# Parts of Q and K after rotation: places of their own, three stores per block for six, first loads given out on two queues

## What is computed

```python
Q = rope((x @ qw).reshape(b, s, 16, 8)); K = rope((x @ kw).reshape(b, s, 16, 8))
V = (x @ vw).reshape(b, s, 16, 8)
score = einsum('bhqd,bhkd->bhqk', Q, K) / sqrt(8) - 1e10 * (1 - causal)
x = layernorm(x + merged(softmax(score - max) @ V) @ ow)
gates = top2_of_softmax(x @ router_w + router_b)       # four experts
x = layernorm(x + sum_e gates[e] * ((silu(x @ w1[e]) * (x @ w3[e])) @ w2[e]))
```

## Time and profile before

| | us |
|---|---|
| median of 3 runs | 496.91 (495.39 to 498.34) |
| the profiled execution's own time | 497.89 |
| its span in the trace | 496.2 |
| PE busy in the span | 416.2 (84%) |
| DVE busy | 313.3 (63%) |
| ACT busy | 267.1 (54%) |
| POOL busy | 190.2 (38%) |

### The profile page before, as it was taken

The page is one execution under the profiler, slowest core; times in us unless marked ns, Lnnn a source line. Parts: engine busy times, 40 slices in busy tenths (PEclk is TensorE's granted clock), DMA queues, the critical chain, the costliest instruction groups (busy, mean ns, idle before and its releaser), DMA issues.

```text
span 496.2 us, 7475 instructions
## 1 busy us (share of the span) xinstructions
PE 416.2 (84%) x2397; PEld 209.4 (42%) x2420; DVE 313.3 (63%) x1027; ACT 267.1 (54%) x377; POOL 190.2 (38%) x255
## 2 busy tenths in 40 slices
PE   5715473899898998989989888989999999999992
PEld 2302310222223222232222322327888788788781
DVE  3526374687887878878778786333556756765844
ACT  1220300557556576575755757676665575565560
POOL 3631320205215152151431513224565574665662
PEclk9957555799999999999999999889999999999996
DMA  6644544021122121221212100000000000000000
GB/s 230 190 125 120 159 100 122 13 63 47 20 65 50 47 61 24 65 49 40 60 33 64 41 3 0 3 0 1 2 0 2 21 1 1 22 1 2 22 0 21
DMA packets 46198, 23.47 MB, mean 47 GB/s; under 512 B 30320, under 2 KB 43248, under 8 KB 46160
## 3 DMA queue, kind: packets, MB, share of 16 engines
q1 hardware_dynamic: 46160, 23.00, 17.6%
HBM read 14.21 MB, written 8.59 MB: 46 GB/s over the span
## 4 chain that ended last, share of the span: by engine, by line
PE 58%; DVE 17%; SPq 7%; DMA 6%; ACT 5%; issue 4%; POOL 2%; POOLq 0%; DVEq 0%; ACTq 0%
PE o_bank L1055 12%; PE t_bank L1123 8%; PE bank L1123 8%; PE t_bank L1134 8%; DVE maxima L789 7%; PE t_bank L1038 6%; PE bank L1015 6%; PE small_bank L1015 3%; DMA q_op<-max_rows 3%; SPq L408 3%; DVE mg_w L785 2%; DVE mg_t L785 2%; DVE x_w L785 2%; SPq L367 2%; ACT num L628 2%
## 5 line engine op out<-in xcount | busy, mean ns | idle before, releaser
L628 ACT ACTIVATE num<-t_bank 128x1024 f32<-128x1024 f32 (+2 forms) x160 | 145.1, 939 | 110.1 <-PE t_bank L1038 108.8
L549 POOL TENSOR_TENSOR hid_lo<-num,q_op 128x512 fp32r<-128x512 f32 x64 | 83.0, 1300 | 60.9 <-ACT q_op L684 59.7
L518 POOL TENSOR_SCALAR_AFFINE_SELECT num<-num 128x512 f32<-128x512 f32 x64 | 40.3, 636 | 145.6 <-ACT num L628 145.5
L1015 PE MATMUL bank<-k_op,q_op 128*128 128x512 bf16 (+7 forms) x241 | 74.4, 338 | 22.8 <-DMA k_op<-k_scratch 10.8
L1055 PE MATMUL o_bank<-num,v_op 128*32 128x512 f32 (+3 forms) x768 | 84.5, 513 | 1.1
L1038 PE MATMUL t_bank<-q_op,k_op 64*128 64x512 bf16 (+3 forms) x384 | 59.8, 339 | 11.9 <-DMA q_op<-max_rows 10.2
L684 ACT ACTIVATE q_op<-num 128x512 fp32r<-128x512 f32 x64 | 40.5, 632 | 45.1 <-DVE num L916 44.7
L789 DVE TENSOR_REDUCE maxima<-bank 128x1 f32<-128x512 f32 x85 | 58.4, 688 | 7.9 <-PE bank L1015 4.5
L785 DVE CUSTOM_DVE_ANT_0 mg_t<-bank,resid 128x320 f32<-128x320 f32 (+6 forms) x85 | 37.9, 446 | 23.2 <-PE bank L1015 14.4
L1015 PEld LDWEIGHTS bank<-k_op,q_op 128*128 128x128 bf16 x255 | 23.2, 98 | 67.3 <-DVE maxima L789 20.8
L1038 PEld LDWEIGHTS t_bank<-q_op,k_op 64*128 64x128 bf16 x384 | 16.0, 93 | 76.6 <-issue 46.3
(11 more groups left out here) (132 smaller groups left out, 640.8 us busy)
## 6 DMA issues: line engine op xcount, KB each, us to landing
k_op<-k_scratch SPq DMA_DIRECT2D x32, 128.0 KB, 2.3
q_op<-q_scratch SPq DMA_DIRECT2D x64, 51.0 KB
q_scratch<-rope_part SPq DMA_DIRECT2D x24, 128.0 KB, 2.4
k_scratch<-rope_part SPq DMA_DIRECT2D x24, 128.0 KB, 2.4
w_raw<-in_w_all SPq DMA_DIRECT2D x6, 512.0 KB, 4.1
xT<-in_x_feat SPq DMA_DIRECT2D x4, 256.0 KB, 5.4
k_scratch<-k_op SPq DMA_DIRECT2D x4, 256.0 KB
q_op<-max_rows SPq DMA_DIRECT2D x64, 3.0 KB
```

Source lines behind the costliest of these rows:

```text
L518: pool.affine_select(out=tile, in_=tile, compare_op=ALU.is_ge, fill=0.0, base=0, pattern=[[0, GH], [1, P]], channel_multiplier=-1)\
L549: pool.tensor_tensor(hid_lo[:, m % HB, :], hid[:, m % HB, :], hid_hi[:, m % HB, :].bitcast(F32), ALU.subtract).then_inc(f_lo, 1)
L628: act.activation(num[:, t % PB, :, off:CH].rearrange("p (k i) t -> p i k t", i=2)[:, :, h:h + each, :], t_bank[k % TB][:, :, 0:each * (CH ...
L1015: pe.matmul(ring(s, step)[:, 0:width], q_op[u][:, pr, j, :, :].rearrange("p i q -> p (i q)"), k_op[u][:, pr, lo:lo + width], start=True, s ...
```

## The change

The three parts of each of the 8 blocks get places of their own, 24 in all, in the memory of `num` (three of its four slots), so no part waits for a store of an earlier block. ACT waits for all stores before the first exponential writes there. In DRAM the scratch tensors are laid out as (head and width) x product x token. The products of one part are then a slice with a step, and one DMA with a repeated source stores all copies of a part: three stores per block for six, of 3, 2 and 1 copies.

The rows of ones no longer go through DRAM: POOL fills both K buffers whole with ones, and the loads of K bring 48 rows for each head, four DMAs for two. The loads of Q bring 48 rows for 51. For groups 0 and 1 the rows of maxima are zero from the memset; from group 2 on each load of a head has a second DMA that brings three rows of zeros. The memset of the second Q buffer moves behind the last part, a memset of the second K buffer stands behind it, and the loads of group 1 wait for that.

For the first chunk, SP loads Q of two heads, and ACT hands out the loads of K and of the other two heads, behind part 1 of block 3. `STEADY` is now written out as a string of letters; the list of steps that comes out is the same, step for step.

```diff
-Q_PART = (0, 0, 1, 1, 2, 0)
-K_PART = (0, 1, 0, 1, 0, 2)
+Q_AT = ((2, 5, 1), (1, 6, 4), (0, 1, 1))
+K_AT = ((0, 3, 1), (3, 6, 2), (4, 5, 1))
...
-STEADY = stage_plan(True, True)
+STEADY = steady_plan(STEADY_ORDER)
...
-        q_dram = nc.dram_tensor("q_scratch", (B * H, QROWS, S), BF16).ap()
-        k_dram = nc.dram_tensor("k_scratch", (B * H, HR, S), BF16).ap()
+        q_dram = nc.dram_tensor("q_scratch", (B * H * DH, PRODUCTS, S), BF16).ap()
+        k_dram = nc.dram_tensor("k_scratch", (B * H * DH, PRODUCTS, S), BF16).ap()
+        z_dram = nc.dram_tensor("zeros", (PARTS, S), BF16).ap()
...
-        rope_part = [sb(f"rope_part{r}", [P, 2, CH], BF16) for r in range(PARTS)]
+        rope_part = num[:, 0:PB - 1, :, :].rearrange("p i h t -> p (i h t)").bitcast(BF16)\
+            .rearrange("p (n r t) -> p n r t", n=2 * CHUNKS, r=PARTS)
...
+        def load_q(eng, n, u, c, heads):
+            for h in heads:
+                pr, i = divmod(h, 2)
+                at = (n * GH + h) * DH
+                eng.dma_start(q_op[u][i * HR:i * HR + KROWS, pr, c * NB:(c + 1) * NB, i, :],
+                              q_dram[at:at + DH, :, c * CH:(c + 1) * CH].rearrange("d r t -> (d r) t"))\
+                    .then_inc(q_loaded[u][c], 16)
+                if n > 1:
+                    eng.dma_start(q_op[u][i * HR + KROWS:i * HR + QROWS, pr, c * NB:(c + 1) * NB, i, :],
+                                  z_dram[:, c * CH:(c + 1) * CH]).then_inc(q_loaded[u][c], 16)
+
+        def load_k(eng, n, u, c):
+            for h in range(GH):
+                pr, i = divmod(h, 2)
+                at = (n * GH + h) * DH
+                eng.dma_start(k_op[u][i * HR:i * HR + KROWS, pr, c * CH:(c + 1) * CH],
+                              k_dram[at:at + DH, :, c * CH:(c + 1) * CH].rearrange("d r t -> (d r) t"))\
+                    .then_inc(k_loaded[u][c], 16)
...
-                for part in range(PARTS):
+                for part, (first, end, step) in enumerate((Q_AT, K_AT)[is_k]):
+                    copies = len(range(first, end, step))
                     sp.wait_ge(part_ready[part], n + 1)
-                    for r, of in enumerate(K_PART if is_k else Q_PART):
-                        if of == part:
-                            sp.dma_start(dram[heads, r * DH:(r + 1) * DH, cols], rope_part[part][:, n % 2, :])\
-                                .then_inc(parts_stored[n % 2], 16)
+                    sp.dma_start(dram[b * P:(b + 1) * P, first:end:step, c * CH:(c + 1) * CH],
+                                 rope_part[:, n, part, :].unsqueeze(1).broadcast_to([P, copies, CH]))\
+                        .then_inc(parts_stored[ch], 16)
...
+            for n in range(3):
                 store(n)
-                if n == 2 * NC - 2:
-                    sp.wait_ge(zeros_stored, 16 * (1 + B * H // ones))
-                    stored(1)
-                    load_q(0, 0, 0)
-                    load_k(0, 0, 0)
-            stored(NC)
-            load_q(0, 0, 1)
-            load_k(0, 0, 1)
+            sp.wait_ge(parts_stored[0], 2 * PARTS * 16)
+            load_q(sp, 0, 0, 0, range(2))
+            for n in range(3, 2 * NC):
+                store(n)
+            sp.wait_ge(parts_stored[1], 2 * PARTS * 16)
+            load_q(sp, 0, 0, 1, range(GH))
+            load_k(sp, 0, 0, 1)
             for n in range(2 * NC, 2 * CHUNKS):
                 store(n)
-            sp.wait_ge(ops_filled, 3)
+            sp.wait_ge(ops_filled, 4)
...
-            pool.memset(k_op[0][:, 0, :], 1.0).then_inc(ops_filled, 1)
+            pool.memset(k_op[0][:, :, :], 1.0).then_inc(ops_filled, 1)
...
-                if n == 1:
-                    pool.memset(q_flat[1][:, :].bitcast(F32), 0.0).then_inc(ops_filled, 1)
             for n in range(2 * CHUNKS - 2, 2 * CHUNKS):
                 third_part(n)
+            pool.memset(q_flat[1][:, :].bitcast(F32), 0.0).then_inc(ops_filled, 1)
+            pool.memset(k_op[1][:, :, :], 1.0).then_inc(ops_filled, 1)
...
+                if n == 4:
+                    act.wait_ge(parts_stored[0], 2 * PARTS * 16)
+                    act.wait_ge(ops_filled, 2)
+                    load_k(act, 0, 0, 0)
+                    load_q(act, 0, 0, 0, range(2, GH))
```

More of the change, by code:

```diff
@@ L148, in stage_plan, with steady_plan @@
     return [(*step, next(uses)) if step[0] in ("MROWS", "NORM") else step for step in plan]
+STEADY_ORDER = ("tsssssmtsssptsssntsptsssptsssptssstssspmtsssstsspntssstsssptsstsssptstssptsstssptptp")
+def steady_plan(order):
+    s_units, small = iter(S_UNITS), iter([("MROWS", NC - 1), ("MROWS", 0)])
+    norms = iter([("NORM", NC - 1), ("NORM", 0)])
+    t_units = iter([(*u, 0) for u in T_UNITS[T_END[0]:]] + [(*u, 1) for u in T_UNITS[:T_END[0]]])
+    tiles, use, plan = iter(T_TILES), iter(range(len(order))), []
+    for letter in order:
+        if letter == "s":
+            plan.append(("S", *next(s_units)))
+        if letter == "t":
+            plan.append(("T", *next(t_units)))
+        if letter == "p":
+            c, kt = next(tiles)
+            plan.append(("PV", c, kt))
+            if kt == TI * (c + 1) - 1:
+                plan.append(("OCOPY", c))
+        if letter == "m":
+            plan.append((*next(small), next(use)))
+        if letter == "n":
+            plan.append((*next(norms), next(use)))
+    return plan + [("END",)]
 PROLOGUE = stage_plan(True, False)
-STEADY = stage_plan(True, True)
+STEADY = steady_plan(STEADY_ORDER)
+assert [sum(x[0] == k for x in STEADY) for k in ("S", "T", "PV", "MROWS", "NORM")] == [NS, NT, NPV, 2, 2]
 LAST = stage_plan(False, True)
@@ L293, in transformer_block @@
         part_ready = [sem(f"part_ready{r}") for r in range(PARTS)]
-        parts_stored = [sem(f"parts_stored{i}") for i in range(2)]
+        parts_stored = [sem(f"parts_stored{i}") for i in range(CHUNKS)]
         v_proj, v_cleared, v_copied = (sem(n) for n in ("v_proj", "v_cleared", "v_copied"))
@@ L370, in stored @@
-            def stored(chunks):
-                for i in range(2):
-                    sp.wait_ge(parts_stored[i], STORES * 16 * chunks)
-            for n in range(2 * NC):
-                store(n)
-                if n == 2 * NC - 2:
-                    sp.wait_ge(zeros_stored, 16 * (1 + B * H // ones))
-                    stored(1)
-                    load_q(0, 0, 0)
-                    load_k(0, 0, 0)
-            stored(NC)
-            load_q(0, 0, 1)
-            load_k(0, 0, 1)
+                    sp.dma_start(dram[b * P:(b + 1) * P, first:end:step, c * CH:(c + 1) * CH],
+                                 rope_part[:, n, part, :].unsqueeze(1).broadcast_to([P, copies, CH]))\
+                        .then_inc(parts_stored[ch], 16)
@@ L388, in _ @@
             for c in range(NC):
-                load_q(1, 1, c)
-                load_k(1, 1, c)
-            stored(CHUNKS)
+                load_q(sp, 1, 1, c, range(GH))
+                load_k(sp, 1, 1, c)
+            for ch in range(NC, CHUNKS):
+                sp.wait_ge(parts_stored[ch], 2 * PARTS * 16)
+            sp.wait_ge(zeros_stored, 16)
             for dst, src in ((wo[:, :], ow), (rw[:, :], router_w),
@@ L423, in stage @@
                         sp.wait_ge(t_ready, NT * n + NT)
-                        load_q(s + 1, v, 1)
-                        load_k(s + 1, v, 1)
+                        load_q(sp, s + 1, v, 1, range(GH))
+                        load_k(sp, s + 1, v, 1)
             for s, plan in enumerate(STAGES):
@@ L588, in second_part @@
                 act.wait_ge(rest_ready, n + 1)
-                if n >= 2:
-                    act.wait_ge(parts_stored[n % 2], STORES * 16 * (n // 2))
-                act.activation(rope_part[1][:, n % 2, :], roped[:, n % 2, :], ACT.Copy).then_inc(part_ready[1], 1)
+                act.activation(rope_part[:, n, 1, :], roped[:, n % 2, :], ACT.Copy).then_inc(part_ready[1], 1)
             for n in range(2 * CHUNKS):
@@ L599, in _ @@
                 act.wait_ge(roped_ready, n + 1)
[L600 to L602 removed]
+                act.activation(rope_part[:, n, 0, :], roped[:, n % 2, :], ACT.Copy).then_inc(part_ready[0], 1)
                 if n >= 1:
                     second_part(n - 1)
+                if n == 4:
[3 more added lines that the diff above has]
+                    load_q(act, 0, 0, 0, range(2, GH))
             copy_v(2)
@@ L607, in _ @@
             copy_v(3)
+            for ch in range(CHUNKS):
+                act.wait_ge(parts_stored[ch], 2 * PARTS * 16)
             act.sem_inc(t_exped, TB)
```

44 lines of the change are left out of this document (12 added, 32 removed).

## The result

| | before | after |
|---|---|---|
| median of the runs, us | 497.62 (495.39 to 498.48, 4 runs) | 481.02 (480.16 to 481.17, 4 runs) |
| ratio | | 0.9669, 95% interval 0.9633 to 0.9706 |
| the profiled execution's own time | 497.89 | 480.89 |
| first `S` matmul / turn of the maxima | 36.37 / 65.12 | 31.92 / 56.27 |
| first `T` matmul | 85.56 | 70.42 |

The changed kernel is faster by 16.6 us; the forecast was 482.0. Of the 17.0 us between the two profiled executions, 15.1 lie ahead of the first `T` unit and 1.9 behind it.

A forecast was written before the change was run, and what follows sets the result against it. Bounds: the prologue's block chain through stores with SP's queue behind it, and SP at steady stage ends. 497.89 profiled - 13.4 (prologue) - 2.0 (stage ends) = 482.5, median forecast 482.0; range 476 to 495, chance 0.62.

The forecast's parts named there:

- What bounds the kernel: Prologue: block chain through stores, with SP's queue behind it; steady stages: SP last at each end, 2.4 us of waits over six.
- Part 1: Prologue, rope chain on POOL and ACT without store waits: 3.66 us a block, where the trace had about 4.8.
- Part 2: Prologue, first loads: ACT's six DMAs take 3.0 us at SP's prices; first `S` matmul at 33.0, 3.4 us earlier.
- rival (b): Prologue gives less: ACT's DMAs at 1.0 us each, or loads of Q at half their old price; 489 us, chance 0.12.
- Part 3: Prologue, first `S` unit to maxima: last third part 11.4 us earlier, 3.7 of uncovered memsets, turn at 57.4, 7.7 earlier.
- Part 4: Prologue, SP's queue: sixteen group 1 loads take 8.0 us; first `T` unit at 72.1 instead of 85.56, 13.4 us gained.
- Part 5: Loads SP hands out ending six steady stages: 5.3 us instead of 5.8; of PE's 2.4 us of waits, 2.0 counted gained.
- excess-increment rule: Steady stage end: issuing sequencer makes excess semaphore increments itself; zeros would cost as the maxima's DMAs, adding 1.6 us a block.
- (a): Rival, steady stage ends: zeros at 0.74 and loads of Q at 0.68 lose 1.8 us per stage; 496.5 us, chance 0.15.
- (c): Rival, slower: loads of Q keep 1.27, zeros cost 0.74; six stages +24.6, prologue -7.6, 515 us; chance 0.07.
- (d): Rival, prologue: new places do nothing because DMA engines limit the stores; 492 us, chance 0.04.
- 8 us of store waits: Prologue: share of the 11.4 us earlier end of block 7's third part, from store waits that stood behind the first `S` unit.

The follow-up runs named there:

- first experiment: Kernel before with each 51-row load of Q split into one of 48 rows and one of 3, nothing else changed: 487.84 us, ratio 0.9784.
- second experiment: Kernel after, but ACT again waits before part 0 of block n until the stores of block n-2 have landed: 481.04 us, ratio 0.9645.

## Why the prediction was right, and where not

| what is in the kernel (Q in loads of 48 rows but for the last line) | us | ratio | first `T` |
|---|---|---|---|
| own places, new layout, three stores, two queues (after) | 481.0 | 0.9669 | 70.42 |
| own places, new layout, six stores, two queues | 480.9 | 0.964 | 69.38 |
| own places, new layout, three stores, SP alone | 480.3 | 0.9617 | 69.84 |
| own places, old layout, six stores, two queues | 480.4 | 0.9636 | 71.44 |
| waits for stores, new layout, three stores, two queues | 481.0 | 0.9645 | 70.10 |
| waits for stores, new layout, six stores, two queues | 481.7 | 0.9665 | 71.63 |
| waits for stores, new layout, three stores, SP alone | 483.2 | 0.9688 | 72.79 |
| waits for stores, new layout, six stores, SP alone | 484.6 | 0.9707 | 75.08 |
| waits for stores, old layout, six stores, SP alone | 488.0 | 0.979 | 78.54 |
| the kernel before with the load of Q split | 487.8 | 0.9784 | 78.17 |
| the kernel before, 51 rows | 497.6 | | 85.56 |

- **What bounds the kernel** was read rightly: a chain through the stores, a queue on SP beside it, and SP last at the end of each steady stage. The first experiment shortens the second and takes away the third and gains 10.8 us; the table's rows from 488.0 to 481.0 are the first, with what stands ahead of the stores in SP's queue.
- **Part 1, the rope chain.** 3.66 us a block forecast, 3.82 measured. The adds of blocks 2 to 5, forecast at 17.6, 21.3, 24.9 and 28.6, came at 16.94, 21.03, 24.86 and 28.68. Two terms are off: POOL's add of block 2 took 1.53 instead of 1.26, and from a third part to the add behind it it is 1.30 us (23.56 to 24.86), where 1.19 was taken. The reading of why the old chain took 4.8 was right in its mechanism (a landing of 2.4 us): with that landing and no waits for it, part 0 comes every 3.8 us.
- **Part 2, ACT's DMAs.** Forecast from 27.4 to 30.4 at SP's prices, measured 26.22 to 29.44, each 0.36 to 0.66 us. They begin 1.2 us earlier than forecast because ACT's queue hands them out while ACT still has part 1 of block 3 (26.69) ahead of it. Part 0 of block 5 was forecast 3 us late for them; it came at 29.98, as the chain brings it, and only a copy of V stood behind them. The first `S` matmul was forecast at 33.0 and came at 31.92. That half of rival (b) falls.
- **Part 3, up to the maxima.** Third part of block 7 done at 50.46 (51.4 forecast), memsets 3.6 us on the path (3.7), turn at 56.27 (57.4). The experiment with the memsets ahead confirms the place: the turn comes 4.3 earlier.
- **Part 4, SP's queue.** A load of Q takes 0.51 in a row (0.55 taken, between 0.47 and 1.27), one of K 0.465 (0.45). All sixteen take 7.7 us (8.0 forecast; 12.1 before, for twelve). SP is through at 61.7 (63.1), the first `T` matmul at 70.42 (72.1). The gain of the prologue is 15.1 us where 13.4 were forecast; the missing 1.7 are the first `S` matmul's 1.1 and the rest SP's. That the 48 rows are what makes the load cheap was argued from the share; the split load shows it. The step from the profiled execution to the median was set at 1 us in the text and at 0.5 in the sum; it came out at 0.1 the other way. Of the distance between 482.5 and the 480.89 profiled, nearly all is the prologue's.
- **Part 5, the END block.** 5.3 us forecast, 4.7 measured: 0.31 for Q, 0.35 for zeros (0.33 forecast), 1.71 for four K. The gain of 2.0 is 1.9. The excess-increment rule of the Trainium skill (Perfetto Trace Analysis, "DMA Instruction — HWDGE (DVE, Sync)"), as it was weighed there beside the row of the maxima's DMAs, would have put the zeros at 0.74; the trace has 0.35, so here the rule gives no price that shows. What goes with 0.74 to 0.76 is three rows from SBUF: the maxima's DMAs, and the zeros as soon as they come from there. For stores of 128 rows, also from SBUF, it does not hold: six take 2.94 us.
- **The rule on the number of DMA engines** (the Trainium skill, DMA: Bandwidth & Descriptors, "Why a DMA increments its semaphore by 16 and not by 1") gives 3 for 51 rows and 16 for 48. The trace agrees on the first (a share of 0.19). For 48 rows, shares of 0.34 in the first experiment and of 0.43 to 0.58 in the prologue after rule out three engines, but none of them shows all sixteen busy.
- **Rivals.** (a) rested on zeros at 0.74. The experiment with zeros from SBUF is that rival built: an END block of 6.8 us, 1.0 over the old 5.8, and the steady part from first to last `T` matmul 252.2 us, 5.7 over the old 246.5, so 0.95 for each stage. The rule that each stage loses what the block is over 5.8 held; (a) was wrong only in its prices. Its sum has a slip: at 0.68 for a load of Q the prologue gains 12.4, not 12.2, and the time would be 496.3. (c) falls with the 48-row load. (d), the places do nothing, was given 0.04, for a reason (the DMA engines as the limit) that is wrong: the same bytes went out in 3.8 us a block. The new places nevertheless do nothing for this kernel's time, and the reason for that, what the other edits do for the same chain, was not among the rivals.

**What the prediction did not see** is in the table. It put 8 us of store waits into the sum as the places' doing. The waits did go, and the table prices them only in company: own places and the second queue together take 488.0 to 480.4, with six stores and the old layout. But with the waits kept, the new layout takes 3.4 us off 488.0, and the second queue 2.9 more (481.7; the first `T` matmul comes 3.5 and 3.4 earlier); the 0.7 left for the three stores is within the scatter. The other edits make own places needless, and where own places stand, going back to six stores, or to SP alone, or to six stores and the old layout costs nothing. The total came out right because the sum followed the chain as a whole; my expectation for the second experiment, which priced a part of it by itself, was wrong by 3 us. Its working error is small: landing behind the last store takes 1.9 us instead of 2.4 with the new layout, so a block is held 0.4 us, not 1.0. All of that is lost ahead of block 5, and from block 6 on the chain stands for DVE anyway: in the kernel after, POOL's adds of blocks 6 and 7 wait 2.60 and 3.21 us for DVE's copy.

Not settled: the equality of 488.0 and 487.8 hides two differences that may cancel. The kernel with all edits back still has its memsets late (the first `T` matmul 3.3 us later, as measured in the kernel after), and it neither stores nor loads the rows of ones. No run has either of them alone on the kernel before. Nor was own places alone built on the kernel with the split load (old layout, six stores, SP alone): that it would do the work of the other three is inferred from the rows above.

## What to carry to other kernels

Look at the DMA share of a stretch in which one kind of load runs alone: 0.19, three of sixteen engines, was the largest thing to gain here, and splitting the load of 51 rows into 48, a multiple of 16, and 3 got it with two lines. When several edits all shorten one chain, take them back together as well as one by one; each alone may show nothing while all together are worth 7 us. And before a step is moved behind the last work of an engine, ask what is queued behind that: two memsets moved there made the first `T` matmul 3.3 us later.

## What the runs showed of the hardware

- Loads of 51 x 8 pieces of 128 bytes moved at a DMA share of 0.19, three of 16 engines, and held the queue for 1.0 to 1.27 us each; 48 rows of it take 0.31 to 0.51, and the other three rows 0.35 or less.
- Handing out a DMA into three rows of 8 pieces took 0.35 us from DRAM and 0.76 from SBUF on the same queue in the same place.
- A store of 128 KB landed in 1.8 to 1.9 us when it wrote 128 rows of one product, in 2.4 when it wrote 16 heads times 8 rows; six of them in a row were handed out in 2.94 and 3.76 us.
- ACT's queue handed out the same loads at SP's price, 0.36 to 0.66 us each.
